# A repaired unit order (one table load counted per change) and shifted tokens made by products with identity matrices, in an eight-pair Mamba, expert, attention and window-attention kernel

## The chip, the cores and the metric

The kernel runs on one core of one Trainium2 chip. The metric is the device time in microseconds, the median of several executions. TensorE is called PE (its weight loads PEld), VectorE DVE, ScalarE ACT, GpSimd POOL and SyncE SP.

## The reference

A batch of 16 sequences of 256 tokens with 128 features passes two blocks. Cut to what matters:

```python
x = L0_attn_x                        # (16, 256, 128), float32
xn = layernorm(x)
x = x + mamba(xn) + moe(xn)          # selective scan (256 channels, 16 states); 8 experts, top 1
xn = layernorm(x)
x = x + geodesic_attention(xn)       # 16 heads of 8; softmax-like weights from arccos of cosines
      + window_transformer(xn)       # 2 layers, 8 heads of 64, window 64

def shift_token(t):                  # used twice in each layer of window_transformer
    t1, t2 = split(t, 2, axis=-1)    # 64 and 64 features
    t2 = pad(t2, one row of zeros ahead)[:-1]
    return concatenate([t1, t2], axis=-1)

def layer(x):
    h = shift_token(x); q, k, v = split(h @ wqkv)      # <- the shift that is changed
    x = x + window_attention(l2norm(q) * qs, l2norm(k) * ks, v) @ wo
    h = layernorm(shift_token(x)) * lg + lb
    a, g = split(h @ w1 + b1); return x + (a * gelu(g)) @ w2 + b2
```

## The kernel before

The 16 sequences are worked in 8 pairs of 512 tokens. The work is cut into units such as ("g_tan", pair, half, step): one stage of the computation on one pair or one sequence, issued on up to four engines. Names that begin with e are the experts, m the Mamba scan, f the join and second layernorm, g the geodesic attention; the units without a prefix (shift, qkv, norm, qn, heads, score, pt, rsum, pv, on, wo, ln, ln2, lnT, up, gelu, hid, down) are one window layer on one sequence. Pair 7's layers are 14 and 15, each with halves 0 and 1, one sequence each.

The order in which each engine meets the units is settled when the program is built. `schedule()` plays the units through a model of the five engines: `STAGES` holds the planner's own durations of a unit on each engine, `LATER` and `STREAM` add a wish (earlier or later) by the unit's name and by its stream (Mamba pair 3, say), and a free engine takes the ready unit with the lowest wish. On ACT a unit whose table of functions isn't loaded pays `SWITCH` in that choice and `LOAD_TIME` in the model's time. The resulting lists are then issued in order on each engine; semaphores alone set the times on the chip. All units of all pairs share eight PSUM banks, which the planner gives out too. What the planner believes has no other effect on the chip than the order and the banks.

ACT needs four tables: logarithm with exponential (most units), SILU (`m_in`), sigmoid with arctan (`g_tan`), GELU (`gelu`). `use()` at line 844 issues a load where the table changes. `g_tan` is Tanh then Arctan:

```python
use(SIG, GELU, SILU)       # loads the first of these unless one of them is there
a.activation(at, at, ACT.Tanh, scale=0.25)      # L1398
use(SIG)
a.activation(at, at, ACT.Arctan)                # L1401
```

The unit `shift` makes a layer's first operand, the shifted tokens with features on partitions: PE transposes the two 128-token tiles of a sequence (line 849, from `xn` in the first layer of a pair, `xd` in the second), and ACT copies them from PSUM to `hT1` in three instructions (lines 1431 to 1433): the 64 unshifted features, one column of zeros, the 64 others one token later. The `qkv` products (line 1153) read `hT1`. `m_scan` (line 1579) is the Mamba scan on DVE, 16 for each pair; `m_turn` (line 1357) is ACT's last copy of a pair's Mamba sums, two for each pair.

Of the kernel before, what the change touches and what calls it, by code (L numbers as in the profile page):

```python
# [10 lines left out]
P = 128  # L11
# [60 lines left out]
    "g_sub": [("POOL", 2.36)], "g_tan": [("ACT", 3.86)], "g_pow": [("ACT", 5.34)], "g_av": [("DVE", 0.53), ("PE", 1.0)],  # L72
    "g_ev": [("ACT", 0.6)], "g_avT": [("PE", 0.44), ("DVE", 1.05)], "g_oT": [("PE", 0.44), ("ACT", 0.6)],
    "g_out": [("PE", 0.89), ("DVE", 0.68)], "out": [("DVE", 0.69), ("SP", 0.1)],
    "shift": [("PE", 0.22), ("ACT", 0.97)], "norm": [("DVE", 0.17), ("ACT", 0.5)], "qn": [("DVE", 1.22)], "heads": [("PE", 0.88), ("ACT", 1.03)],
    "score": [("PE", 0.62), ("DVE", 0.61)], "pt": [("PE", 1.7), ("ACT", 0.7)], "rsum": [("PE", 0.65), ("ACT", 0.86)], "pv": [("PE", 1.15)], "on": [("DVE", 0.66)],
    "wo": [("PE", 1.83), ("DVE", 0.42)], "ln": [("PE", 0.69), ("DVE", 0.77), ("ACT", 0.54)],
    "ln2": [("DVE", 0.72)], "lnT": [("PE", 0.22), ("DVE", 0.54)], "up": [("PE", 0.86)], "gelu": [("ACT", 1.2)],
# [11 lines left out]
         "norm": "ln", "pt": "ln", "rsum": "ln", "ln": "ln", "m_in": "silu", "g_tan": "tan", "gelu": "gelu"}  # L90
SWITCH = 127.0

LATER = {"down": 17.13, "e_down": 0.92, "e_lg": -1373.3, "e_ln": 621.99, "e_load": -1698.97, "e_place": -129.783, "e_pre": 351.489,
         "e_route": 144.702, "e_scat": 829.618, "e_store": -223.789, "e_tr": -184.595, "e_up": 44.242, "e_xn": -28.591, "e_xt": -830.714,
         "f_ln": 818.98, "f_tr": -1660.36, "f_xn": -118.536, "f_yg": -111.816, "g_av": 89.144, "g_avT": -202.085, "g_ev": -784.392,
         "g_hd": -35.958, "g_ln": 938.103, "g_norm": -59.145, "g_oT": 238.89, "g_out": 718.35, "g_pow": 876.48, "g_qkv": 45.815,
         "g_score": 49.652, "g_sq": 72.566, "g_sub": 570.978, "g_tan": 44.449, "gelu": -343.785, "heads": 43.677, "hid": -127.469,
         "l_weights": 625.975, "ln": -124.928, "ln2": 1.634, "lnT": -15.963, "m_B": -153.424, "m_C": 17.261, "m_bx": 50.752,
         "m_dt": 18.917, "m_du": 21.175, "m_ex": -16.259, "m_fin": 74.245, "m_hc": 137.244, "m_in": -23.847, "m_load": -295.604,
         "m_out": -935.123, "m_scan": 731.575, "m_sum": 14.942, "m_turn": -247.837, "m_weights": -173.243, "m_xp": 895.808,  # L100
         "norm": -15.561, "on": -140.182, "out": 284.565, "pt": -39.622, "pv": 82.873, "qkv": 47.209, "qn": -65.566, "rsum": -2.347,
         "score": -4.24, "shift": -70.641, "up": -71.786, "wo": 25.239, "x_load": 44.744}

STREAM = {("-", 0): 147.932, ("e", 0): -62.078, ("e", 1): 166.105, ("e", 2): -162.027, ("e", 3): 122.427, ("e", 4): 496.972, ("e", 5): -233.745,
# [14 lines left out]

LOADED = [15.0, 24.0]  # L120

# [309 lines left out]
def schedule():  # L431
# [64 lines left out]
    while done < todo:  # L496
        for x in [y for y in waiting if y[0] <= now]:
            waiting.remove(x)
            offer(x[1], 0, now)
        again = True  # L500
        while again:
            again = False
            for e in engines:
                if free_at[e] > now:
                    continue
                best = None
                for x in engines[e]:
                    unit, stage, _ = x
                    if not may(unit, stage):
                        continue  # L510
                    needs = NEEDS.get(unit[0]) if e == "ACT" else None
                    cost = want[unit] + (SWITCH if needs and needs != table else 0)
                    if best is None or cost < best[0]:
                        best = (cost, x, needs)
                if best is None:
                    continue
                unit, stage, _ = x = best[1]
                engines[e].remove(x)
                taken.update(holds(unit)[0].get(stage, []))
                needs_banks = takes_banks(unit)  # L520
                if needs_banks and needs_banks[0] == stage:
                    banks[bank_of(unit)] = choose(unit, needs_banks[1])
                    for m, z in enumerate(banks[bank_of(unit)]):
                        idle.remove(z)
                        before_it[bank_of(unit), m] = held_by.get(z)
                        held_by[z] = (bank_of(unit), m)
                takes = stages(unit)[stage][1]
                if best[2] and best[2] != table:
                    takes += LOAD_TIME * (2 if best[2] == "tan" and table == "ln" else 1)
                    table = best[2]  # L530
                if e == "DVE" and unit[0] in DUAL:
                    takes += max(0.0, pool_until - now)
                    dual_until = now + takes
                if e == "POOL" and unit[0] in POOLED:
                    takes += max(0.0, dual_until - now)
                    pool_until = now + takes
                free_at[e] = now + takes
                plan[e].append(unit)
                line(unit, e).pop(0)
                events.append((now + takes + lands(unit, e), done, unit, stage))  # L540
                done += 1
                again = True
        times = [x for x in free_at.values() if x > now] + [x[0] for x in events + waiting]
        if not times:
            raise ValueError([(e, x[:3]) for e, x in engines.items()])
        now = min(times)
        for x in sorted(y for y in events if y[0] <= now):
            events.remove(x)
            finish(x[2], x[3], x[0])
# [31 lines left out]
def build(nc, d, out):  # L581
    ctx = ExitStack()
    with ctx:
# [263 lines left out]
        def transpose(out_, in_):  # L847
            k = in_.shape[0]
            return t.transpose(out_, in_, ident[0:k, 0:k])  # L849
# [101 lines left out]
        def tensor_program():  # L951
            for u, i, b, k in order(plan, "PE"):
# [183 lines left out]
                elif u == "shift":  # L1136
                    into(unit)
                    if l:
                        t.wait_ge(v_xd[b], n)
                    else:  # L1140
                        t.wait_ge(v_xn, n // LAY + 1)
                    for h in range(2):
                        e = transpose(lb()[:, h * P:(h + 1) * P], (xd if l else xn[n // LAY % 2])[:, 2 * b + h])
                    e.then_inc(p_sh[b], 1)
                    read_by(unit, a_hT[b], n + 1)
                elif u == "qkv":
                    if n == 0:
# [123 lines left out]
        def scalar_program():  # L1271
            for u, i, b, k in order(plan, "ACT"):
# [154 lines left out]
                elif u == "shift":  # L1427
                    a.wait_ge(p_sh[b], n + 1)
                    if n:
                        a.wait_ge(p_pt[b], 4 * n)  # L1430
                    a.activation(hT1[b][0:64], lb()[0:64, 0:L], ACT.Copy)
                    a.activation(hT1[b][64:128, 0:1], one_b[64:128, 0:1], ACT.Copy, scale=0.0)
                    a.activation(hT1[b][64:128, 1:L], lb()[64:128, 0:L - 1], ACT.Copy).then_inc(a_hT[b], 1)
                elif u == "qkv":
                    tt, w = divmod(k, 3)
                    a.wait_ge(p_q[b], 2 * (2 * n + tt) + w // 2 + 1)
# [601 lines left out]
```

## Time and profile before

| what | value |
|---|---|
| median of 3 runs | 2261.49 us (2258.05 to 2261.52) |
| the profiled execution | 2262.57 us, its span 2261.3 us |
| busy PE | 1788.6 us, 79% of the span |
| busy ACT | 1739.7 us, 77% |
| busy DVE | 1697.8 us, 75% |
| busy POOL | 541.0 us, 24% |
| mean granted clock of PE | 0.863 |

A busy share is the time in which the engine had an instruction under way. The span is the profiled execution without the 1.3 us around it. No engine is close to full, so no engine's sum of work alone sets the end: the rest is time in which an engine stands at the head of its list for something that another engine has not done yet.

### The profile page before, as it was taken

How to read it: one execution, taken by the hardware profiler on the slowest of the kernel's cores; microseconds unless marked ns; L12 is line 12 of the kernel's file. 1: busy time of each engine (PE TensorE's matmuls, PEld its weight loads, DVE VectorE, ACT ScalarE, POOL GpSimd, SP SyncE). 2: the span in 40 equal slices, each digit the busy share in tenths (PEclk: the TensorE clock that was granted, in tenths of full speed). 3: DMA queues.
4: the chain of work that ended last, by engine and by line, in shares of the span. 5: the costliest groups of instructions: out<-in, count | busy, mean ns of one | idle time of the engine just before them, and what ended most of it. 6: DMA issues, size and time to landing. Idle time of an engine off the chain costs nothing. (4 is left out here: it accounts for less than half of the span.)

```text
span 2261.3 us, 40539 instructions
## 1 busy us (share of the span) xinstructions
PE 1788.6 (79%) x15282; PEld 1293.3 (57%) x15282; DVE 1697.8 (75%) x2517; ACT 1739.7 (77%) x2887; POOL 541.0 (24%) x270
## 2 busy tenths in 40 slices
PE   3668788998778977788688887886778786779787
PEld 2654566776466654555465565554556464556565
DVE  4878887775999698859976889749984799655552
ACT  2435786857888697887878988977589958887996
POOL 2231122222311222312232222302142121232230
PEclk9687778999889888898788887998988888889888
DMA  6751214350341133114310233013300242000000
GB/s 227 237 170 48 71 38 135 117 147 18 127 136 52 53 117 108 43 39 131 113 39 14 73 122 103 10 49 121 130 21 2 84 141 84 1 1 2 6 1 6
DMA packets 81651, 177.39 MB, mean 78 GB/s; under 512 B 10388, under 2 KB 41940, under 8 KB 81332
## 3 DMA queue, kind: packets, MB, share of 16 engines
q1 hardware_dynamic: 75632, 163.53, 22.4%
q0 software_dynamic: 2816, 7.21, 1.0%
q10 hardware_dynamic: 3012, 4.06, 0.5%
q8 instruction: 125, 2.05, 0.4%
q14 instruction: 66, 0.54, 0.1%
HBM read 161.92 MB, written 12.85 MB: 77 GB/s over the span
## 5 line engine op out<-in xcount | busy, mean ns | idle before, releaser
L1855 POOL TENSOR_TENSOR arena<-arena 128x1024 f32<-128x1024 f32 x128 | 316.3, 2493 | 622.8 <-ACT arena L1392 622.6
L1859 POOL TENSOR_TENSOR arena<-arena,rb 128x1024 f32<-128x1024 f32 x64 | 152.2, 2378 | 866.5 <-DVE rb L1711 866.5
L1579 DVE TENSOR_TENSOR_SCAN ps<-dA,ps 128x1024 f32<-128x1024 f32 x128 | 291.0, 2284 | 1.6 <-ACT dA L1351 1.0
L1153 PE MATMUL ps<-w_l_wqkv,arena 128*128 128x512 f32 x384 | 205.8, 670 | 23.0 <-DVE hB L1587 6.4
L844 ACT ACT_TABLE_LOAD x153 | 196.3, 1283 | 19.3 <-issue 16.6
L1413 ACT ACTIVATE arena<-arena 128x256 f32<-128x256 f32 x512 | 205.3, 402 | 2.0
L1351 ACT ACTIVATE dA<-mv,w_A_log 128x510 f32<-128x510 f32 x256 | 167.8, 711 | 42.2 <-DVE ps L1579 39.1
L1093 PE MATMUL ps<-gqT,gkT 8*128 8x256 f32 x1024 | 164.7, 460 | 38.9 <-DVE arena L1652 16.1
L1652 DVE TENSOR_SCALAR arena<-ps 128x1024 f32<-128x1024 f32 x128 | 155.0, 1217 | 51.3 <-PE ps L1093 50.7
L1573 DVE TENSOR_TENSOR ps<-BC,mv 128x1024 f32<-128x1024 f32 x128 | 181.6, 1425 | 12.9 <-ACT arena L1457 4.1
L849 PE MATMUL ps<-w_ident,arena 128*128 128x128 f32 x623 | 112.1, 326 | 99.5 <-DVE arena L1512 28.6
L1043 PE MATMUL ps<-w_ident,hB 128*128 128x128 f32 x1024 | 162.4, 312 | 28.7 <-DVE hB L1587 28.6
L1043 PEld LDWEIGHTS ps<-w_ident,hB 128*128 128x128 f32 x1024 | 136.5, 162 | 54.4 <-DVE hB L1587 33.2
L1729 DVE TENSOR_REDUCE nmx<-ps 128x4 f32<-128x512 f32 x128 | 87.8, 686 | 97.8 <-PE ps L1181 97.2
L849 PEld LDWEIGHTS ps<-w_ident,arena 128*128 128x128 f32 x623 | 87.2, 169 | 125.0 <-issue 83.2
L1587 DVE TENSOR_TENSOR hB<-ps,BC 128x1024 f32<-128x1024 f32 x128 | 154.4, 1214 | 4.4 <-PE ps L1043 3.6
L1093 PEld LDWEIGHTS ps<-gqT,gkT 8*128 8x128 f32 x1024 | 101.0, 213 | 80.4 <-issue 70.4
L1192 PE MATMUL ps<-arena 64*128 64x192 f32 (+1 forms) x1024 | 118.5, 352 | 35.1 <-DVE rb L1711 13.9
L1390 ACT ACTIVATE arena<-arena,one_b 128x2048 f32<-128x2048 f32 x64 | 127.7, 1996 | 22.8 <-DVE arena L1652 20.9
L1192 PEld LDWEIGHTS ps<-arena 64*128 64x128 f32 x1024 | 92.5, 207 | 83.8 <-issue 49.9
L1153 PEld LDWEIGHTS ps<-w_l_wqkv,arena 128*128 128x128 f32 x384 | 74.4, 211 | 101.9 <-issue 94.1
L1392 ACT ACTIVATE arena<-arena,one_b 128x2048 f32<-128x2048 f32 x64 | 128.2, 2003 | 2.1
(223 smaller groups left out, 4507.7 us busy)
## 6 DMA issues: line engine op xcount, KB each, us to landing
BC<-bc_d SPq DMA_DIRECT2D x224, 512.0 KB, 4.2
BC<-in_experts SPq DMA_DIRECT2D x16, 514.0 KB
arena<-in_experts SPq DMA_DIRECT2D x15, 514.0 KB
mv<-in_experts SPq DMA_DIRECT2D x15, 514.0 KB, 3.4
arena<-in_x SPq DMA_DIRECT2D x8, 256.0 KB, 4.7
xnT_d<-arena SPq DMA_DIRECT2D x8, 256.0 KB, 3.0
hB<-xnT_d SPq DMA_DIRECT2D x8, 256.0 KB, 2.6
x<-in_x SPq DMA_DIRECT2D x8, 256.0 KB, 5.6
```

The costliest lines, as they stand in the source:

```text
L844: a.preload_act_table_set(names[0])
L849: return t.transpose(out_, in_, ident[0:k, 0:k])
L1043: e = t.matmul(lb()[:, tt * P:(tt + 1) * P], hB[k % 2][:, j, tt * P:(tt + 1) * P], ident, is_transpose=True, start=q == j == tt == 0, stop ...
L1093: e = t.matmul(lb(z)[:, kt * L:(kt + 1) * L], gkT[32 * hi:32 * hi + GD, hb, kt * P:(kt + 1) * P], gqT[32 * hi:32 * hi + GD, hb], start=Tru ...
L1153: e = t.matmul(lb(z), hT1[b][:, tt * P:(tt + 1) * P], w_lqkv[:, l, (w + z) * INNER:(w + z + 1) * INNER], start=True, stop=True)
L1192: t.matmul(lb(z)[:, cols], kT[head_rows(z), k, at:at + P], qT[head_rows(z), k, at:at + cols.stop - cols.start], start=kt == 0, stop=False)
L1351: e = a.activation(dA[k % 2][:, j].rearrange("p (s l) -> p s l", s=2)[:, :, 1:], dtv[:, c].rearrange("p (s l) -> p s l", s=2)[:, :, 1:], A ...
L1413: e = a.activation(part, part, ACT.Exp, scale=-3.2, accum_out=vt[m % 2][:, kt, hi, GD + 2:GD + 3])
L1573: v.tensor_tensor(two_banks(unit), Bb[j % 2], bc(du[:, c:c + 1], [P, NG, T]), ALU.mult).then_inc(v_bx, 1)
L1579: v.tensor_tensor_scan(h_, flat2(dA[k % 2]), h_, 0.0, ALU.mult, ALU.add).then_inc(v_scan, 1)
L1652: v.tensor_scalar(cl[m % 2][:, 2 * (k % 2):2 * (k % 2) + 2], two_banks(unit), -1.0 + 1e-7, 1.0 - 1e-7, ALU.max, ALU.min).then_inc(v_gs, 1)
L1855: g.tensor_tensor(la[m % 2][:, half], la[m % 2][:, half], cl[m % 2][:, half], ALU.subtract).then_inc(g_sub, 1)
```

## The change

Three things change. First, `shift` on PE: in place of two transposes there are four products of 64 features by 128 tokens, two with the identity (features 0 to 63) and two with the identity moved by one column, `w_next` (features 64 to 127, one token later), and one product with one column, which adds at token 128 what the first tile's last token owes the second. Second, the zeros and the shift are then in PSUM already, and ACT empties it with a single copy of 128x256. Third, the planner: its durations of `shift` change, it counts one `LOAD_TIME` for any change of table (before, two for one from the logarithm's table to `g_tan`), and `LATER` and `STREAM` have new numbers throughout.

```diff
-    "shift": [("PE", 0.22), ("ACT", 0.97)], ...
+    "shift": [("PE", 0.55), ("ACT", 0.4)], ...

-LATER = {"down": 17.13, "e_down": 0.92, "e_lg": -1373.3, ...
+LATER = {"down": 26.626, "e_down": -47.853, "e_lg": -154.046, ...

                 if best[2] and best[2] != table:
-                    takes += LOAD_TIME * (2 if best[2] == "tan" and table == "ln" else 1)
+                    takes += LOAD_TIME
                     table = best[2]

+                    rows = xd if l else xn[n // LAY % 2]
                     for h in range(2):
-                        e = transpose(lb()[:, h * P:(h + 1) * P], (xd if l else xn[n // LAY % 2])[:, 2 * b + h])
-                    e.then_inc(p_sh[b], 1)
+                        for z, moved in ((0, ident), (1, w_next)):
+                            t.matmul(lb()[head_rows(z), h * P:(h + 1) * P], rows[:, 2 * b + h, 64 * z:64 * z + 64], moved, start=True, stop=True)
+                    t.matmul(lb()[head_rows(1), P:P + 1], rows[:, 2 * b, 64:128], ident[:, P - 1:P], start=False, stop=True,
+                             skip_group_check=True).then_inc(p_sh[b], 1)

-                    a.activation(hT1[b][0:64], lb()[0:64, 0:L], ACT.Copy)
-                    a.activation(hT1[b][64:128, 0:1], one_b[64:128, 0:1], ACT.Copy, scale=0.0)
-                    a.activation(hT1[b][64:128, 1:L], lb()[64:128, 0:L - 1], ACT.Copy).then_inc(a_hT[b], 1)
+                    a.activation(hT1[b], lb()[:, 0:L], ACT.Copy).then_inc(a_hT[b], 1)
```

Lines behind the PE edit stand three higher in the changed kernel (two from ACT's `shift` on to one): the old L1398 is L1401, the old L1484 is L1485.

The new order touches every engine from its first microseconds on. Three places of it follow. The first is on PE, the last `shift` of the program (layer 15, half 1; `xd` is the residual stream of the window layers). Before:

```order
L1181 MATMUL ps<-arena 64x128 x4
L849 MATMUL ps<-w_ident,xd 128x128 x2
L1224 MATMUL ps<-arena 32x192 x2
L1224 MATMUL ps<-PT,arena 32x192 x2
L1224 MATMUL ps<-arena 32x128 x2
```

In the changed kernel:

```order
L1268 MATMUL ps<-w_l_w,arena 128x128 x6
L1145 MATMUL ps<-w_ident,xd 64x128 x4
L1146 MATMUL ps<-w_ident,xd 64x1
L1156 MATMUL ps<-w_l_wqkv,arena 128x512 x6
L1107 MATMUL ps<-arena,vt 32x256 x8
```

The two transposes became four products and a fifth with one column, and the `qkv` products now follow at once, where others stood between.

The second place is on ACT around the last copy of the Mamba sums (`mv<-ps 128x512`, `m_turn` of pair 7), behind which the program holds no Mamba work on ACT. Before:

```order
L1465 ACTIVATE arena<-ps 128x640
L1357 ACTIVATE mv<-ps 128x512
L1439 ACTIVATE arena<-ps 128x1024
L1408 ACTIVATE arena<-arena,one_b 128x2048
L1413 ACTIVATE arena,vt<-arena 128x256 x8
L1465 ACTIVATE PT<-ps 128x640
```

In the changed kernel:

```order
L1466 ACTIVATE arena<-ps 128x640
L1434 ACTIVATE arena<-ps 128x256
L1360 ACTIVATE mv<-ps 128x512
L1393 ACTIVATE arena<-arena,one_b 128x2048
L1395 ACTIVATE arena<-arena,one_b 128x2048
L1425 ACTIVATE avS<-ps 128x512
```

Counted in the whole order, ACT had 361 instructions behind that copy and has 287 now. The difference by kind: 24 fewer of L1413 (104 to 80), 11 fewer with 2048 columns (12 to 10 each of L1390, L1392, L1398 and L1401, 13 to 10 of L1408), 8 fewer table loads (27 to 19), 11 fewer of `shift` (5 times three to 4 of one), and 20 fewer short ones. In the same way DVE has 280 instructions behind its last scan (318 before), and PE 1295 behind its last Mamba sum, line 1043 (1514 before). Over the whole program the table loads are 164 (153 before), and all other instructions of ACT and DVE but those of `shift` are as many as before; PE has 96 more.

The third place is ACT again, the last two `g_tan` pairs (L1398 and L1401) of the program. Before:

```order
L844 ACT_TABLE_LOAD
L1398 ACTIVATE arena<-arena 128x2048
L1401 ACTIVATE arena<-arena 128x2048
L844 ACT_TABLE_LOAD
L1484 ACTIVATE arena<-ps,w_l_b 128x256 x2
L1484 ACTIVATE arena<-ps,w_l_b 87x256
L844 ACT_TABLE_LOAD
L1465 ACTIVATE arena<-ps 128x640
L844 ACT_TABLE_LOAD
L1398 ACTIVATE arena<-arena 128x2048
L1401 ACTIVATE arena<-arena 128x2048
L844 ACT_TABLE_LOAD
```

In the changed kernel (numbers as above):

```order
L844 ACT_TABLE_LOAD
L1401 ACTIVATE arena<-arena 128x2048
L1404 ACTIVATE arena<-arena 128x2048
L1401 ACTIVATE arena<-arena 128x2048
L1404 ACTIVATE arena<-arena 128x2048
L844 ACT_TABLE_LOAD
L1466 ACTIVATE arena<-ps 128x640 x2
L1411 ACTIVATE arena<-arena,one_b 128x2048
```

Here two `g_tan` share one load and the GELU has gone behind them. Over the whole program it is the other way: 25 times two `g_tan` stood together before, 17 times now.

## Rows read from the trace of the kernel before

**Rows 1.** The page: busy time by engine, and two rows by slices

```profile
PE 1788.6 (79%) x15282; PEld 1293.3 (57%) x15282; DVE 1697.8 (75%) x2517; ACT 1739.7 (77%) x2887; POOL 541.0 (24%) x270
...
DVE  4878887775999698859976889749984799655552
ACT  2435786857888697887878988977589958887996
```

**Rows 2.** The page: the chain of work that ended last, by engine

```profile
PE 6%; ACT 6%; DVE 2%; issue 1%; DVEq 0%; ACTq 0%
```

**Rows 3.** Last Mamba scan on DVE, last Mamba copy on ACT: ns, first to last start

```profile
L1579 DVE TENSOR_TENSOR_SCAN ps<-dA,ps x128: 2261/2285/2296, 64.7 to 1910.7; 128x1024 f32<-128x1024 f32 x128
...
L1357 ACT ACTIVATE mv<-ps x16: 574/594/599, 159.5 to 1927.2; 128x512 f32<-128x512 f32 x16
```

**Rows 4.** Busy us (instructions) of PE, PEld, DVE, ACT, POOL; clock; DMA

```profile
0.00:1927.20 1927.20, 1521.96 (x12726) 1100.12 (x12728) 1528.35 (x2209) 1460.78 (x2422) 455.94 (x235) 0.86 0.28 92
1927.20:2261.30 334.10, 266.62 (x2558) 193.21 (x2558) 169.45 (x309) 278.94 (x467) 85.05 (x35) 0.87 0.01 3
...
0.00:1913.00 1913.00, 1508.99 (x12620) 1093.12 (x12620) 1520.92 (x2200) 1452.60 (x2399) 453.58 (x234) 0.86 0.29 92
1913.00:2261.30 348.30, 279.58 (x2662) 200.21 (x2662) 176.88 (x318) 287.12 (x489) 87.41 (x36) 0.86 0.01 3
```

**Rows 5.** Groups on ACT from 1927.2 us on: busy us, mean ns

```profile
L1413 ACT ACTIVATE arena<-arena 128x256 f32<-128x256 f32 x104 | 41.7, 402 | 0.4
L844 ACT ACT_TABLE_LOAD x27 | 34.6, 1283 | 0.5
L1408 ACT ACTIVATE arena<-arena,one_b 128x2048 f32<-128x2048 f32 x13 | 25.9, 1993 | 0.0
...
L1401 ACT ACTIVATE arena<-arena 128x2048 f32<-128x2048 f32 x12 | 22.9, 1910 | 0.4
...
L1465 ACT ACTIVATE PT<-ps 128x640 f32<-128x640 f32 x13 | 9.1, 697 | 2.8 <-PE ps L1202 2.8
```

**Rows 6.** Groups of the whole run: table loads, shift's copies, a 128x256 copy

```profile
L844 ACT ACT_TABLE_LOAD x153 | 196.3, 1283 | 19.3 <-issue 16.6
...
L1470 ACT ACTIVATE arena<-ps 128x256 f32<-128x256 f32 x64 | 24.3, 380 | 24.2 <-PE ps L1212 23.4
...
L1433 ACT ACTIVATE arena<-ps 64x255 f32<-64x255 f32 x32 | 12.1, 378 | 0.4
L1431 ACT ACTIVATE arena<-ps 64x256 f32<-64x256 f32 x32 | 11.8, 368 | 9.8 <-PE ps L849 9.8
...
L1432 ACT ACTIVATE arena<-one_b 64x1 f32<-64x1 f32 x32 | 6.4, 200 | 0.4
```

**Rows 7.** Timeline of PE at a shift: start us, us

```profile
1000.99 0.38 PE L849 MATMUL ps<-w_ident,xn 128*128 128x128 f32 x2
...
1001.65 0.28 PE L1212 MATMUL ps<-arena,one_b 128*32 128x128 f32 x2
1001.67 0.28 PE L1212 MATMUL ps<-PT,one_b 128*32 128x128 f32 x2
1001.76 0.28 PE L1212 MATMUL ps<-arena,one_b 128*32 128x128 f32 x2
```

**Rows 8.** Timeline of ACT near the end, around table loads

```profile
2212.01 1.91 ACT L1401 ACTIVATE arena<-arena 128x2048 f32<-128x2048 f32 x1
2213.94 1.28 ACT L844 ACT_TABLE_LOAD   x1
2215.23 1.19 ACT L1484 ACTIVATE arena<-ps,w_l_b 128x256 f32<-128x256 f32 x3
2216.44 1.28 ACT L844 ACT_TABLE_LOAD   x1
2217.74 0.70 ACT L1465 ACTIVATE arena<-ps 128x640 f32<-128x640 f32 x1
2218.46 1.28 ACT L844 ACT_TABLE_LOAD   x1
```

More of the change, by code:

```diff
@@ L74 @@
     "g_out": [("PE", 0.89), ("DVE", 0.68)], "out": [("DVE", 0.69), ("SP", 0.1)],
-    "shift": [("PE", 0.22), ("ACT", 0.97)], "norm": [("DVE", 0.17), ("ACT", 0.5)], "qn": [("DVE", 1.22)], "heads": [("PE", 0.88), ("ACT", 1.03)],
+    "shift": [("PE", 0.55), ("ACT", 0.4)], "norm": [("DVE", 0.17), ("ACT", 0.5)], "qn": [("DVE", 1.22)], "heads": [("PE", 0.88), ("ACT", 1.03)],
     "score": [("PE", 0.62), ("DVE", 0.61)], "pt": [("PE", 1.7), ("ACT", 0.7)], "rsum": [("PE", 0.65), ("ACT", 0.86)], "pv": [("PE", 1.15)], "on": [("DVE", 0.66)],
@@ L91 @@
 SWITCH = 127.0
[L93 to L102, printed above, removed]
@@ L104 @@
-STREAM = {("-", 0): 147.932, ("e", 0): -62.078, ("e", 1): 166.105, ("e", 2): -162.027, ("e", 3): 122.427, ("e", 4): 496.972, ("e", 5): -233.745,
[14 rows of a table removed]
+LATER = {"down": 26.626, "e_down": -47.853, "e_lg": -154.046, "e_ln": 153.128, "e_load": -413.903, "e_place": 198.432, "e_pre": 372.282,
+         "e_route": 78.833, "e_scat": -133.57, "e_store": 294.029, "e_tr": -401.726, "e_up": 10.066, "e_xn": 93.952, "e_xt": -1039.55,
+         "f_ln": 1106.4, "f_tr": -322.455, "f_xn": 217.43, "f_yg": -10.994, "g_av": 97.117, "g_avT": -642.248, "g_ev": -451.117,
+         "g_hd": -107.765, "g_ln": 1286.07, "g_norm": -120.908, "g_oT": 944.286, "g_out": 190.596, "g_pow": 1280.3, "g_qkv": 64.332,
+         "g_score": 50.079, "g_sq": -142.519, "g_sub": -7.947, "g_tan": 70.185, "gelu": -544.024, "heads": 50.193, "hid": -284.193,
+         "l_weights": -54.396, "ln": -431.199, "ln2": -432.525, "lnT": -137.825, "m_B": 7.171, "m_C": -955.695, "m_bx": 42.085,
+         "m_dt": 96.366, "m_du": 297.038, "m_ex": 43.637, "m_fin": 159.803, "m_hc": 143.75, "m_in": 21.962, "m_load": 701.197,
+         "m_out": -718.386, "m_scan": 2376.5, "m_sum": 25.023, "m_turn": -358.511, "m_weights": 139.751, "m_xp": 1472.38,
+         "norm": -295.405, "on": -852.033, "out": -519.201, "pt": -305.656, "pv": 88.73, "qkv": 44.395, "qn": -533.45, "rsum": -13.76,
+         "score": -11.158, "shift": -205.939, "up": -112.371, "wo": 36.793, "x_load": 100.085}
@@ L120 @@
+STREAM = {("-", 0): -58.238, ("e", 0): -221.022, ("e", 1): 1263.18, ("e", 2): -232.508, ("e", 3): 325.479, ("e", 4): 68.616, ("e", 5): -262.222,
[14 rows of a table added]
 LOADED = [15.0, 24.0]
```

28 rows, old and new, of the table STREAM are left out of this document.

## The prediction

> **What bounds the kernel now.** I read the page first. PE, ACT and DVE are busy 79%, 77% and 75% of the span [rows 1], and the chain that ended last is held by PE 6%, ACT 6% and DVE 2% [rows 2], so it covers only the last stretch and can't be charged with the whole. The reader should see three engines, each a quarter idle, that wait for each other; no single wait is long enough to be named as the bound. What varies is the mix: in the slices DVE stands at 9 up to the middle and falls to 5 and 2 at the end, where ACT stands at 9 [rows 1].
>
> So I looked for the place where the mix changes. The last Mamba scan starts at 1910.7 us and takes 2.3, so it ends at 1913.0; ACT's last copy of Mamba sums starts at 1927.2 [rows 3]. Splitting the run there gives the two regimes [rows 4]. Up to 1927.2 us ACT is busy 1460.78 us, a share of 0.758, and PE 1521.96, or 0.790; up to 1913.0 DVE is busy 1520.92, or 0.795. Behind 1927.2 there are 334.1 us in which ACT is busy 278.94, a share of 0.835, PE 266.62 (0.798), but DVE only 169.45 (0.51). The tail is ACT's, with PE close; DVE, which has all the scans, has little left. An order that brings attention and window work forward, beside the scans, shortens the tail. One that puts it off lengthens it.
>
> **The shift, ACT's part.** Three instructions of 368, 200 and 378 ns fall away, 0.946 us, and one 128x256 copy from PSUM comes, whose nearest row is L1470 with the same shape and 380 ns [rows 6]. That is 0.566 us less for each of 32 shifts: -18.1 us of ACT's work.
>
> **The shift, PE's part.** Two transposes ran in 0.38 us together [rows 7]. The four products aren't in the trace in this form. The nearest row is L1212, products with 128 rows into 32 columns of the array: of four such at 128 columns the first start at 1001.65 and the next set at 1001.76 [rows 7], so neighbours in different columns of the array go side by side, a set every 0.11 us. If the two halves pair up like that, two sets take what two transposes took, and only the one-column product is new, some 0.04 us: +1.3 us over 32. If they don't, two more steps of 0.11 and one of at most 0.11 come: 0.33 us each, +10.6. They write different columns of the array as L1212 does, so I take a value near the lower end, 3 us. On the path of one shift (0.38 and 0.95 before qkv can start, against 0.4 to 0.7 and 0.38) it can't lose; I book nothing for it beyond ACT's busy time, as another unit of PE usually stands ready in between.
>
> **The planner's count of loads.** The edit to LOAD_TIME removes no load from the chip. Already now g_tan is preceded by one load, and Arctan by none. What reaches the chip is the new numbers' order. It has 164 loads for 153: 11 at 1.283 us [rows 6] are +14.1 us of ACT's work. With the shift, ACT's total goes by -4.0 us: alone, no change worth measuring.
>
> Here a rule speaks against the change. In the trace a load costs its own duration and no more: it starts at 2216.44, lasts 1.28, and the next instruction starts at 2217.74; the three at 2213.94 to 2218.46 are all like that [rows 8]. The Trainium skill, page ScalarE: Activation LUTs, section What ACT_TABLE_LOAD costs, adds a drain of about 1.38 us to each change of set, 2.66 us in all, and advises grouping by set. By that price, an estimate from that page, the 11 loads would be 29 us and not 14. The trace does not agree.
>
> **The tail.** Behind ACT's last Mamba copy the order holds 361 instructions before and 287 after. The itemised difference: 24 of L1413 at 0.402 are 9.6 us; 8 loads at 1.283 are 10.3; 11 with 2048 columns at 1.91 to 1.99 are 21.5 [rows 5]; the shifts fall from 5 x 0.946 to 4 x 0.38, 3.2 us [rows 6]; the 20 short ones lie between the 0.2 us of the smallest row and 1.0, with L1465 at 0.697 the commonest [rows 5, 6], and I take 0.55 each, 11.0. Together 55.6 us. ACT's tail is then 278.9 - 55.6 = 223.3 us busy, and at the same share of 0.835 it lasts 267.4 in place of 334.1: **-66.7 us**.
>
> **What is paid ahead of it.** That work has not gone; it stands beside the scans. ACT's part before its last Mamba copy grows by 55.6 - 4.0 = 51.6 us; at its share of 0.758, +68 us. DVE has 280 instructions behind its last scan for 318; at 176.88 us for the 318 [rows 4] that is 21 us moved forward, at 0.795 +27 us. PE has 1295 behind its last sum for 1514; 266.62 us [rows 4] scaled so is 38.5 us, with the shift's 3 some 42, at 0.790 +53 us. Were ACT alone to set the pace ahead, the scans would end 68 us later; were DVE, 27. The shares ahead are nearly alike on all three, none of them sets the pace alone, so I take the mean of the three, (68 + 27 + 53) / 3 = **+49 us**.
>
> **Sum.** 49 - 67 = -18 us against the profiled 2262.6 gives 2244.6. That execution lay 1.1 us above the median of the runs, so I forecast 2243. Its own range, from the spread of that mean and from 3 to 10.6 us on PE, is 2230 to 2256.
>
> **Rivals.**
> 1. *Much faster, because the shares themselves rise.* The planner's picture of ACT was wrong before: 35 changes from the logarithm's table to g_tan were counted double, some 45 us of loads that the chip never does (35 x 1.283) [rows 6]. With a true picture, units may be placed where they are really ready. If ACT ahead of the tail were at 0.775 in place of 0.758, its 1512.4 us there would take 1951, and with 267 the total would be 2218. For it: the 0.835 of the tail shows that ACT can be denser. Against: the waits on the chip are a few microseconds each and come from PE, DVE and PSUM as much as from ACT. 2205 to 2229.
> 2. *Slower: ACT sets the pace ahead, and PE the tail.* ACT takes the 11 more loads and the moved work, and the scans end +68 us later. In the tail PE is next after ACT: its 266.6 us shrink to 228, at 0.798 286 us, or -48. The sum is +20, 2282. It decides when ACT holds up the scans: each scan needs m_ex from ACT (L1351). What speaks for it is that 145 loads stand ahead of the last Mamba copy where 126 stood, in the stretch where ACT has to serve the scans; what speaks against it is that DVE is denser than ACT there. It turns from gain to loss when the scans end more than 67 us late. 2266 to 2290.
> 3. *No change*: ACT alone sets both stretches. +68 - 67 is +1, 2262, within 0.2% (4.5 us, about what a measurement of this kernel can tell from none).
>
> By the page's price above, the 19 more loads ahead of the tail and 8 fewer behind would make rival 2 the likelier one: the 11 x 1.38 would add 15 us to my forecast, 2258. The rows give it no support, and I leave it 3 in 100, within rivals 2 and 3.
>
> **How the numbers follow.** The forecast 0.50; rival 1 0.17; rival 2 0.20; rival 3 0.13. Faster is the forecast with rival 1, less the little of it above 2257: 0.66. Same 0.13, slower 0.21. The range is 2208 to 2272: it leaves out about 0.05 of rival 1 below and 0.13 of rival 2 above.
>
> **What would show it.** In the changed profile: L1434 at about 380 ns 32 times, and L1145 sets that start 0.11 us apart (right) or single products 0.11 apart each (PE's cost of 10.6). 164 loads of 1283 ns, each followed at once by the next instruction. ACT's busy time near 1736 us, DVE's unchanged. The last L1580 scan near 1950 us with 267 us behind ACT's last L1360, in place of 334; a scan end beyond 1995 us makes the forecast wrong and rival 2 right, one at 1920 or earlier speaks for rival 1. ACT's share ahead of that copy tells the two apart: 0.76 for the forecast, 0.775 or more for rival 1, 0.75 or less for rival 2. The forecast is also wrong if the tail's share falls: its 223 us busy of ACT stretched beyond 290.

## Result, and the profile after

The changed kernel takes 2146.4 us in the median (2141.5 to 2160.8, 4 runs) against 2261.3: a ratio of 0.951, 95% interval 0.946 to 0.955. The forecast was 2243; the side was right, the size was missed by far, and the time lies 62 us below the range.

The page of the changed kernel, busy time by engine and the same two rows by slices as in [rows 1]:

```profile
PE 1730.9 (81%) x15538; PEld 1268.6 (59%) x15538; DVE 1684.1 (79%) x2517; ACT 1727.3 (81%) x2834; POOL 541.9 (25%) x270
...
DVE  4968998766899799877997699878997699777363
ACT  2534798858996478898998999888999898978986
```

The work is nearly what it was: ACT 12 us less, DVE 14 less, PE 58 less though it has more instructions. The span lost 121 us: on ACT 109 and on DVE 107 of them are time in which the engine stood idle, on PE 63. The 58 us that PE is busy less go with its clock: the granted clock was 0.863 before and is 0.894, and 1788.6 x 0.863 / 0.894 is 1727. The reader should compare the middle of the rows: ACT stood mostly at 7 and 8 there and now stands mostly at 8 and 9.

Last starts of the Mamba scan and of ACT's last Mamba copy, as in [rows 3]:

```profile
L1580 DVE TENSOR_TENSOR_SCAN ps<-dA,ps x128: 2259/2284/2296, 64.4 to 1852.8; 128x1024 f32<-128x1024 f32 x128
...
L1360 ACT ACTIVATE mv<-ps x16: 578/594/603, 161.4 to 1865.8; 128x512 f32<-128x512 f32 x16
```

The split at that copy, and at the end of the last scan, as in [rows 4], columns the same:

```profile
0.00:1865.80 1865.80, 1507.55 (x13352) 1108.91 (x13356) 1534.30 (x2251) 1503.29 (x2466) 471.28 (x240) 0.89 0.29 95
1865.80:2140.20 274.40, 223.32 (x2190) 159.66 (x2190) 149.82 (x266) 223.98 (x369) 70.58 (x30) 0.90 0.01 3
0.00:1855.10 1855.10, 1499.24 (x13254) 1102.55 (x13255) 1528.15 (x2237) 1492.71 (x2440) 471.28 (x240) 0.89 0.29 95
```

The tail lasts 274 us with ACT busy 224.0; the prediction had 267 with 223.3. Ahead of it ACT does 1503.3 us of work, as predicted (1512), but in 1866 us, where I had 1976: a share of 0.806 and not 0.765. All of the miss is there. The other two engines are denser there too: PE has 0.808 for 0.790, DVE up to the end of its last scan 0.824 for 0.795.

The longest waits of ACT before (us in total, times, longest):

```profile
ACT arena L1439 <- PE ps L1153: 55.5, 30, 6.3
ACT arena L1465 <- PE ps L1202: 39.9, 20, 7.8
ACT dA L1351 <- DVE ps L1579: 39.1, 25, 4.3
ACT PT L1465 <- PE ps L1202: 36.9, 23, 4.2
ACT arena L1457 <- PE ps L849: 34.6, 25, 4.7
```

and of the changed kernel:

```profile
ACT PT L1466 <- PE ps L1205: 43.9, 24, 5.3
ACT arena L1466 <- PE ps L1205: 33.4, 17, 7.0
ACT arena L1440 <- PE ps L1156: 27.5, 23, 2.7
...
ACT dA L1354 <- DVE ps L1580: 21.6, 19, 2.6
...
ACT arena L1458 <- PE ps L849: 19.8, 15, 4.8
```

The lines stand one to three higher there (L1439 is L1440). None of the five vanished; three about halved (55.5 to 27.5, 39.1 to 21.6, 34.6 to 19.8), one fell a little (39.9 to 33.4) and one grew (36.9 to 43.9). Together they give 60 of the 109 us of idle time that ACT lost. A better order looks like this: many waits of one to five microseconds, fewer in number and shorter each.

### The profile page after: what moved, and what is told of

Read it like the earlier page. It is cut to its first block and busy times, and to the rows that moved or that the text cites. A ratio compares the mean times of both kernels' runs of the same rounds, so it can differ in the third digit from the quotient of the medians.

```text
span 2140.2 us, 40998 instructions
## 1 busy us (share of the span) xinstructions
PE 1730.9 (81%) x15538; PEld 1268.6 (59%) x15538; DVE 1684.1 (79%) x2517; ACT 1727.3 (81%) x2834; POOL 541.9 (25%) x270
## 5 line engine op out<-in xcount | busy, mean ns | idle before, releaser
L844 ACT ACT_TABLE_LOAD x164 | 210.4, 1283 | 18.8 <-issue 15.9
L1156 PE MATMUL ps<-w_l_wqkv,arena 128*128 128x512 f32 x384 | 196.5, 639 | 23.2 <-DVE hB L1588 6.5
L1354 ACT ACTIVATE dA<-mv,w_A_log 128x510 f32<-128x510 f32 x256 | 168.7, 713 | 21.9 <-DVE ps L1580 21.6
L1093 PE MATMUL ps<-gqT,gkT 8*128 8x256 f32 x1024 | 155.2, 439 | 38.5 <-DVE arena L1653 15.1
L1653 DVE TENSOR_SCALAR arena<-ps 128x1024 f32<-128x1024 f32 x128 | 154.8, 1216 | 34.0 <-PE ps L1093 33.4
L1043 PE MATMUL ps<-w_ident,hB 128*128 128x128 f32 x1024 | 150.2, 295 | 23.7 <-DVE hB L1588 18.4
L1043 PEld LDWEIGHTS ps<-w_ident,hB 128*128 128x128 f32 x1024 | 126.4, 153 | 50.2 <-issue 25.2
L1093 PEld LDWEIGHTS ps<-gqT,gkT 8*128 8x128 f32 x1024 | 96.1, 204 | 75.3 <-issue 66.4
L1393 ACT ACTIVATE arena<-arena,one_b 128x2048 f32<-128x2048 f32 x64 | 127.7, 1995 | 10.5 <-DVE arena L1653 9.0
L1395 ACT ACTIVATE arena<-arena,one_b 128x2048 f32<-128x2048 f32 x64 | 128.2, 2003 | 2.1
L1411 ACT ACTIVATE arena<-arena,one_b 128x2048 f32<-128x2048 f32 x64 | 127.6, 1994 | 0.1
```

Of the source, the lines that this page charges most:

```text
L844: a.preload_act_table_set(names[0])
L1043: e = t.matmul(lb()[:, tt * P:(tt + 1) * P], hB[k % 2][:, j, tt * P:(tt + 1) * P], ident, is_transpose=True, start=q == j == tt == 0, stop ...
L1093: e = t.matmul(lb(z)[:, kt * L:(kt + 1) * L], gkT[32 * hi:32 * hi + GD, hb, kt * P:(kt + 1) * P], gqT[32 * hi:32 * hi + GD, hb], start=Tru ...
L1156: e = t.matmul(lb(z), hT1[b][:, tt * P:(tt + 1) * P], w_lqkv[:, l, (w + z) * INNER:(w + z + 1) * INNER], start=True, stop=True)
L1354: e = a.activation(dA[k % 2][:, j].rearrange("p (s l) -> p s l", s=2)[:, :, 1:], dtv[:, c].rearrange("p (s l) -> p s l", s=2)[:, :, 1:], A ...
```

## Experiments

Sixteen kernels ran, each beside the kernel before on the same chip. In these later comparisons the kernel before took 2249 to 2252 us, so the ratios, not the microseconds, compare across them: the changed kernel's 0.9506 is 2138 us there.

**e1, one line.** The planner of the kernel before counts one load for each change of table; nothing else.

```diff
-                    takes += LOAD_TIME * (2 if best[2] == "tan" and table == "ln" else 1)
+                    takes += LOAD_TIME
```

> The kernel before with a single edit: the planner counts one LOAD_TIME for every change of table, as the changed kernel does. The old wishes (LATER, STREAM), the old shift and its old planner costs stay. The order differs from the kernel before from the first window layer on; it has 155 table loads (before 153, changed kernel 164). Theory FIT (the wishes in LATER and STREAM are fitted to one exact set of planner costs, the old wishes to one load per change; any other cost scrambles the order): this line alone gives most of the gain, 2130 to 2165 us. Theory SEARCH (the new wishes are simply better ones, and the old ones are as good as they get): a small change either way, 2240 to 2275. Theory SHIFT (the gain comes from the shorter shift): 2255 to 2270, no change.

Measured: 2180.8 us, ratio 0.968 (0.965 to 0.972). This line reaches the chip only through the order (and the PSUM banks that the planner gives out with it), and it gives two thirds of the gain with the old wishes and the old shift. SEARCH and SHIFT are out as sole causes; FIT is right in kind, 16 us short of its range. The split at the end of the last scan, columns as in [rows 4]:

```profile
0.00:1884.10 1884.10, 1517.65 (x12838) 1104.87 (x12839) 1534.80 (x2223) 1486.47 (x2458) 464.01 (x239) 0.86 0.29 94
1884.10:2185.90 301.80, 246.44 (x2446) 177.76 (x2444) 167.61 (x295) 251.35 (x432) 73.09 (x31) 0.89 0.01 3
```

Both parts shrank: the scans end at 1884 (before 1913), the tail is 302 us (before 348). ACT's share ahead of that end is 0.789 (before 0.759), though its work in the whole run is the same within 2 us.

**e2, the shift alone.** The program edit of `shift` as in the change, the planner untouched.

```diff
-                        e = transpose(lb()[:, h * P:(h + 1) * P], (xd if l else xn[n // LAY % 2])[:, 2 * b + h])
+                            t.matmul(lb()[head_rows(z), h * P:(h + 1) * P], rows[:, 2 * b + h, 64 * z:64 * z + 64], moved, start=True, stop=True)
...
+                    a.activation(hT1[b], lb()[:, 0:L], ACT.Copy).then_inc(a_hT[b], 1)
```

> The kernel before with the program edit of shift alone (four products and a one-column product on PE, one copy on ACT); the planner is untouched, so every unit stands where it stood before. Theory SHIFT: a clear gain, 2140 to 2200. Theories FIT and SEARCH: ACT has 18 us less to do but none of it binds everywhere, so 0 to 15 us less, 2246 to 2261.

Measured: 2247.3 us, ratio 0.9985 (0.9969 to 1.0002): no difference that can be told from none.

**e3, the order alone.** The changed kernel with the old transposes and three copies in the program, the inverse of e2's edit, every unit where the changed kernel has it.

> The changed kernel with the old shift in the program (two transposes, three copies), in the changed kernel's order. Theory SHIFT: back near 2260. Theories FIT and SEARCH: nearly all of the gain stays; ACT has 18 us more to do in a denser order, 2148 to 2166.

Measured: 2142.4 us, ratio 0.9515 (0.9487 to 0.9544). The whole gain stays. ACT is busy 1749.3 us here, 22 more than in the changed kernel, at a cost of 2 us, give or take 12. The split at the end of its last scan:

```profile
0.00:1856.30 1856.30, 1500.04 (x13038) 1095.46 (x13039) 1530.26 (x2237) 1511.85 (x2494) 468.96 (x240) 0.89 0.30 95
```

With the old shift ACT has a share of 0.814 here.

**e4, a nudge.**

```diff
-"hid": -284.193, ... "qkv": 44.395,
+"hid": -284.193, ... "qkv": 44.695,
```

> The changed kernel with one wish moved by 0.3 of over 2000 (LATER of qkv 44.395 to 44.695), which the planner turns into another order from the second window layer on (179 table loads for 164; 150 units of ACT behind the last Mamba copy for 132). All planner costs stay as true as in the changed kernel. Theory FIT: the gain is a property of this one order, not of the costs, and a neighbour is an ordinary order: 2215 to 2270. Theory TRUE PICTURE (the gain comes because the planner now counts loads as the chip does): the neighbour keeps most of it, 2145 to 2185.

Measured: 2220.4 us, ratio 0.988 (0.984 to 0.993), as FIT had it. The same costs, one wish moved by 0.3, and three quarters of the gain are gone. The split at the end of its last scan:

```profile
0.00:1869.00 1869.00, 1482.67 (x12772) 1082.54 (x12772) 1514.10 (x2200) 1475.74 (x2404) 455.55 (x234) 0.88 0.30 94
1869.00:2213.00 344.00, 276.75 (x2766) 201.07 (x2766) 180.39 (x318) 274.29 (x446) 85.99 (x36) 0.89 0.01 3
```

The scans end early here too, but with less beside them, and the tail is as long as in the kernel before (348). So an order can win one of the two stretches and lose the other. The nudged order also has 15 more table loads (179 for 164), some 19 us more work on ACT; the loss is some 85 us, so they are the smaller part of it.

**e5 to e7, more work on one engine at a time**, order of the changed kernel.

```diff
                     use(LN_EXP)
+                    a.preload_act_table_set(LN_EXP)          # e5, in g_pow
...
+                    if k % 2 == 0:                           # e6, in g_score on DVE
+                        v.tensor_reduce(idle_out[:, m], two_banks(unit), AX.X, ALU.max)
...
-                    for kt in range(2):                      # e7, in g_score on PE
+                    for kt in (0, 1, 0, 1)[:4 if k % 2 == 0 else 2]:
```

> The changed kernel with a second, needless load of the logarithm's table ahead of each of the 64 g_pow units; the order is unchanged. ACT has 64 x 1.283 = 82 us more to do. Theory MEAN (the prediction's step: the three engines share the pace and one engine's work counts a third ahead of the tail): 82/3 divided by 0.8, about +30 to +45 us, 2175 to 2190. Theory ACT BINDS: +75 to +100, 2220 to 2245. Theory SLACK (ACT's idle fifth absorbs it): under +20, below 2165. By the Trainium skill's price of 2.66 us for a change of set (page ScalarE: Activation LUTs, section What ACT_TABLE_LOAD costs), an estimate from that page, ACT would have 170 us more and the time would pass 2260.

> The changed kernel with one more DVE reduction over 128x1024 elements in PSUM (about 1.2 us, nothing reads its result) ahead of the clamp in each of the 64 even g_score units; order unchanged. DVE has about 78 us more. Theory MEAN: +25 to +45, 2172 to 2190. Theory DVE BINDS ahead of the tail: +70 to +90. Theory SLACK: under +20.

> The changed kernel with the four score products of each of the 64 even g_score units issued twice (same operands, same place); order unchanged. PE has some 64 x 0.5 to 1.0 = 32 to 64 us more. Theory MEAN: +12 to +30, 2158 to 2176. Theory PE BINDS: +40 to +70. Theory SLACK: under +12.

Measured: e5 2198.8 us (ratio 0.979, 0.976 to 0.982), e6 2186.9 (0.973, 0.971 to 0.975), e7 2190.4 (0.975, 0.973 to 0.978). Only 57 of e5's 64 loads are in the program: in the other seven places `use()` issues a load of the same table directly ahead, and the trace has one load there, not two. The extra work in e5 and e6:

```profile
L1410 ACT ACT_TABLE_LOAD  x57: 1283/1283/1283, 258.8 to 2159.2; - x57
```

```profile
L1655 DVE TENSOR_REDUCE idle_out<-ps x64: 1192/1216/1226, 214.8 to 2093.3; 128x2 f32<-128x1024 f32 x64
```

For e7 the group of the repeated products is compared with the same group in e5, which ran at nearly the same granted clock (0.882, e7 0.881):

```profile
L1093 PE MATMUL ps<-gqT,gkT 8*128 8x256 f32 x1024 | 160.5, 450 | 34.3 <-DVE arena L1654 12.6 <-DVE rb L1713 6.8 <-DVE hB L1589 6.4
```

```profile
L1093 PE MATMUL ps<-gqT,gkT 8*128 8x256 f32 x1536 | 228.9, 450 | 30.2 <-DVE arena L1653 8.6 <-DVE rb L1712 8.3 <-DVE hB L1588 5.8
```

| | work added, us | time added, by the ratios, us | quotient |
|---|---|---|---|
| e5 ACT | 57 x 1.283 = 73 | 64 | 0.9 |
| e6 DVE | 64 x 1.216 = 78 | 50 | 0.6 |
| e7 PE | 228.9 - 160.5 = 68 | 55 | 0.8 |

(The intervals of the ratios make each time uncertain by some 12 us, the quotients by 0.2.) MEAN, the step of the prediction, expected 0.33 / 0.8 = 0.4 for each; only e6 comes near it. None binds alone, none has slack. Together they are 2.3: in the dense order a delay on any engine is handed on to the others, which the picture of three independent shares can't give. Two limits: all three ran at a mean granted clock of 0.881 where the changed kernel had 0.890, and some 9 us of each time go with that (worked out under "Open"). And the quotient is that of work put at this place: e3's 22 us more on ACT, in the shifts, cost 2 us, give or take 12.

**e8 and e11, the count changed in mid-program.** The kernel before with two loads counted only behind (e8) or only ahead of (e11) the middle of the planner's time.

```diff
-LOAD_TIME * (2 if best[2] == "tan" and table == "ln" else 1)
+LOAD_TIME * (2 if best[2] == "tan" and table == "ln" and now > 1066 else 1)     # e8; e11: now <= 1066
```

> The kernel before, where the planner counts one load per change in the first half of its own time and two for logarithm to g_tan in the second. Its order is that of e1 up to the middle and goes its own way behind it. Theory FIT (each stretch is as good as its match to the wishes): half of the loss of the kernel before against e1, about 2215. Theory TAIL (what matters is how the last pair ends): all of the loss is there, 2240 to 2260. Theory FRONT (the loss is made early and stays): 2180 to 2195, as e1.

> The mirror of e8: the kernel before, with two loads counted for logarithm to g_tan in the first half of the planner's time and one in the second. The order is that of the kernel before up to the middle. Theory FIT, in which it is the whole chain of choices that was fitted: a true count behind a scattered first half meets wishes that were fitted to other states and gives little, 2220 to 2250. Theory STRETCH (each half is as good as its own count): half of the gain of e1, about 2215.

Measured: e8 2231.3 us, ratio 0.993 (0.991 to 0.996); e11 2237.1, 0.995 (0.993 to 0.997). e8 keeps e1's whole first half and only a fifth of e1's gain. In e11 a true count in the second half behind the old first half is worth 12 us of e1's 69. So the two halves don't add up: 18 and 12 us for 69. STRETCH, TAIL and FRONT fall, TAIL by 9 us only. FIT had e11 right, but for e8 it had about 2215, and the time came 16 us above that: FIT says which orders are poor, not by how much.

**e12, the shift in the order of e1.** e1's line and e2's edit together.

> The order of e1 (old wishes, one load per change, old planner costs of shift) with the new shift in the program. It says what the shift edit is worth in a dense order. Theory SHIFT COUNTS WHEN DENSE (ACT's work counts three quarters there, by e5): 0.75 x 18 us less on ACT and some microseconds more on PE, 5 to 12 us below e1, 2168 to 2176. Theory SHIFT NEVER COUNTS: 2178 to 2184. e1 stood 40 us above the changed kernel though both orders came of fitted wishes; if this run closes that gap, the gap was the shift.

Measured: 2151.2 us, ratio 0.958 (0.954 to 0.961), by the ratios 24 us below e1 (0.968), give or take 11. The time lies below both expected ranges. The same edit is worth 0.15% in the order before, 0.1% in the changed kernel's (e3 against it) and 1.1% in e1's, the last two give or take 0.5%. By e5's quotient 18 us less work on ACT would give 16, which the interval allows; in e3 the same work cost next to nothing. What it removes here isn't settled. In the profiled executions the granted clock of PE is 0.881 where e1 has 0.868, and PE is busy 1753 us for 1764.

**e9, e10, e13 to e16, the wishes searched anew.** The numbers in `LATER` and `STREAM` were changed at random, one to three at a time, some 18,000 times, and kept where the planner's own end came earlier. e9 keeps the kernel before's program; the others have the changed kernel's program and start from the old wishes. e9, e13 and e14 count two loads from logarithm to g_tan, e10, e15 and e16 one:

```diff
-LATER = {"down": 17.13, "e_down": 0.92, ...
+LATER = ...        # as searched
...
-                    takes += LOAD_TIME                       # e13, e14
+                    takes += LOAD_TIME * (2 if best[2] == "tan" and table == "ln" else 1)
```

> The kernel before, old shift and the false count (two loads from logarithm to g_tan) kept; only the numbers in LATER and STREAM were searched anew, some 18,000 random changes of one to three wishes kept where the planner's own end came earlier. 161 table loads. Theory TRUE PICTURE (the planner must count loads as the chip does): the false count still misplaces 37 of them, 2225 to 2260. Theory FIT (the count itself does little harm; what the kernel before lacks is wishes fitted to the count it uses): most of the gain comes, 2155 to 2200.

> The changed kernel (new shift, one load per change) with other wishes: the old ones of the kernel before as the start, and the same number of random changes as in e9. Its first order, without the search, would be as scattered as that of e4. Theory FIT: within 1 per cent of e9 and near the changed kernel, 2150 to 2190. Theory TRUE PICTURE: 2150 to 2190 too, but 2 per cent or more below e9. Theory LUCK (the changed kernel's order happened to suit the chip, another one doesn't): 2200 to 2240.

> As e10 (changed kernel's program, planner costs of the new shift, old wishes searched anew with as many random changes), but the planner counts two loads from logarithm to g_tan. It differs from e10 in that count and what the search made of it alone; 156 loads, the count is false at 33 places. Theory TRUE PICTURE: like e9, 2200 to 2235. Theory LUCK (e9 was an unlucky order, and orders spread by a per cent either way): 2140 to 2180.

> A second search of the same kind as e13 with other random changes; 153 loads, false at 34 places. TRUE PICTURE: 2200 to 2240. LUCK: anywhere from 2140 to 2225, unlike e13.

> A second search of the kind of e10 (one load per change); 156 loads. TRUE PICTURE: 2135 to 2165. LUCK: anywhere from 2135 to 2225.

> A third search of the kind of e10, whose planner's end stayed 0.8 per cent later than that of e10; 156 loads. TRUE PICTURE, with the chip following the planner's end: 2150 to 2185. LUCK: anywhere from 2135 to 2225.

| wishes | count of loads | ratio to the kernel before | planner's own end, us |
|---|---|---|---|
| fitted: the changed kernel | true | 0.951 (0.946 to 0.955) | 2134 |
| e1, the old wishes | true | 0.968 (0.965 to 0.972) | 2132 |
| searched anew: e10 | true | 0.951 (0.948 to 0.955) | 2148 |
| e15 | true | 0.970 (0.965 to 0.976) | 2152 |
| e16 | true | 0.966 (0.963 to 0.969) | 2165 |
| searched anew: e13 | false | 0.965 (0.963 to 0.967) | 2175 |
| e14 | false | 0.982 (0.979 to 0.985) | 2186 |
| e9 | false | 0.989 (0.986 to 0.992) | 2191 |
| not fitted to the costs: e4 | true | 0.988 (0.984 to 0.993) | 2223 |
| e8, e11 | half and half | 0.993, 0.995 | 2219, 2209 |
| the kernel before | false | 1 | 2248 |

The last column is no measurement: it is the time at which `schedule()` of each kernel, played without the chip, finishes its last unit. It shows what the runs alone leave open, that the old wishes do fit a planner that counts one load. With them and that count the planner ends at 2132 us, as early as with the changed kernel's wishes (2134); with the count of two at 2248. Only part of this is the time of the loads that the chip never does: the order of the kernel before, played once more with one load each, still ends at 2227. The searched orders end between 2132 and 2191, the others at 2209 or later. On the chip a single order lies between 10 us below and 48 us above that end (e10, e1), so the column ranks the two kinds of order and not single ones.

e13 alone refutes the strict TRUE PICTURE: with the count false at 33 places a searched order still is 3.5% faster. e15 and e16 refute that a true count ensures the best: the chip spreads 2% over orders that the search left near each other (e10 and e15, whose ends lie 4 us apart). e9 and e10 alone would have misled: 4% apart, it looked like the count. With all in, orders with a true count average 0.961 (five), with a false one 0.978 (three), those whose wishes were not fitted 0.988 and up. That the false count costs a further percent or two after a search is likely but, with e13 below e15, not shown.

For the last scan, e10 and e9 differ as the changed kernel and the kernel before did. e10:

```profile
L1557 DVE TENSOR_TENSOR_SCAN ps<-dA,ps x128: 2261/2286/2296, 65.2 to 1852.9; 128x1024 f32<-128x1024 f32 x128
```

and e9:

```profile
L1556 DVE TENSOR_TENSOR_SCAN ps<-dA,ps x128: 2261/2286/2296, 66.4 to 1916.5; 128x1024 f32<-128x1024 f32 x128
```

## Why the prediction was right or wrong

**The split into two regimes and the tail: right.** ACT's work behind its last Mamba copy was forecast at 223.3 us and is 224.0, its share there 0.835 and is 0.816, its length 267 and is 274.

**"What is paid ahead of it": wrong, the step that failed.** The prediction's +49 us there was in truth -61: ACT's last Mamba copy came at 1866 us, before at 1927. I took each engine's share ahead of the tail as a constant (0.758, 0.795, 0.790), divided the moved work by it and took the mean. The moved work was right within 10 us, the shares were not constants: ACT's is 0.806, and the copy comes at 1866 where the sum gave 1976. A share is a result of the order, and the order was replaced. e1 and e3 show that the order alone moves it, with the work as it was (ACT's share up to the end of the last scan: 0.759 before, 0.789 in e1, 0.814 in e3); e5 to e7 show the second fault, that engines which wait for each other don't each carry a third.

**"The edit to LOAD_TIME ... What reaches the chip is the new numbers' order": half wrong.** It removes no load, true, but the line reorders the program with the numbers as they were, and that alone is 3.2% (e1). The wishes and the costs are one thing: the old wishes fit a planner that counts one load, as its own end shows (2132 us). The kernel before paired them with a count of two and so had an order that was not fitted to its costs. The diff and `use()` showed the contradiction; I counted it as 45 us of loads that the planner only believes in, in rival 1. I also never played `schedule()` for its end: 2248 against 2134 us would have spoken for a large gain before any run. That this difference of 115 us is also the measured one is luck, as e1 shows, which the planner has 48 us too early. A smaller misreading: Arctan is preceded by no load in 60 of 64 places, not in all; in four Tanh runs with another table, and the load stands between the two.

**Rival 1 was the case that came, for half of its reason and at a third of its size.** I gave it 0.17 and 2205 to 2229. The shares did rise, but less through the true count as such than through fitted wishes (e4 with true costs 0.988, e13 with a false count 0.965).

**The shift.** ACT's copy: 0.38 us expected, and so it is (0.36 to 0.42). On PE the timeline of the changed kernel shows one of the first shifts, at the upper level of the clock (granted 1.00 in this stretch), and the last one, at the lower level (0.50); start, us:

```profile
294.31 0.66 PE L1145 MATMUL ps<-w_ident,xd 128*64 128x128 f32 x8
294.81 0.23 PE L1146 MATMUL ps<-w_ident,xd 128*64 128x1 f32 x2
...
2054.13 1.12 PE L1145 MATMUL ps<-w_ident,xd 128*64 128x128 f32 x8 [0.60 <-DVE xd L1768]
...
2055.04 0.32 PE L1146 MATMUL ps<-w_ident,xd 128*64 128x1 f32 x2
2055.46 0.37 ACT L1434 ACTIVATE arena<-ps 128x256 f32<-128x256 f32 x1
2055.85 1.28 ACT L844 ACT_TABLE_LOAD   x1
```

Four products are eight entries, two each, where a transpose of float32 is one. The halves do go side by side (their entries start 6 ns apart), but there are four sets and not two. From the first start to the last end a shift takes 0.72 us at the upper level, where two transposes took 0.38 to 0.44. So PE's price is the upper bound of some 0.33 us for each shift, 10.6 in all, and not the 3 us that I took; for my 0.04 us for the product with one column no row spoke, and it is two entries as well. It made no difference to the sum: in the order before (e2) and the changed kernel's (e3) the whole edit of the shift is worth nothing that can be measured; in e1's (e12) it is worth more.

**Table loads.** 164 came, at 1283 ns each. By the Trainium skill, page ScalarE: Activation LUTs, section What ACT_TABLE_LOAD costs, a change of set takes 2.66 us in all. The trace of the changed kernel doesn't agree: behind 151 of the 163 loads that follow on other work the next instruction starts within 1.31 us of the load's start, and the load itself mostly starts 18 ns behind the end of the instruction before it. So 2.66 us for each has no support here. e5's loads change no set, so they don't test that price; 57 of them added 64 us, 1.1 each, and the profile shows the next instruction at once:

```profile
258.76 1.28 ACT L1410 ACT_TABLE_LOAD   x1
260.06 2.00 ACT L1412 ACTIVATE arena<-arena,one_b 128x2048 f32<-128x2048 f32 x1
```

**Rivals 2 and 3**: my mark for a loss was a last scan that ends beyond 1995 us; it started at 1853, which is beyond my mark for rival 1 (1920 or earlier) too. The 11 more loads were real, 14 us, and small beside the 109 us of idle time that ACT lost.

**Open.** The granted clock goes with the time: 0.863 before, 0.868 in e1, 0.859 in e9, 0.894 in the changed kernel, 0.897 in e10. It goes with it inside one kernel too, where the order is the same: over 118 executions (the changed kernel, e1 to e16 and the kernel before beside them), each set against the mean of its own kernel, 0.01 more clock comes with 10 us less time (8 to 12). The changed kernel's four executions have a mean clock of 0.890, the 39 later ones of the kernel before 0.867. At that rate 23 of some 111 us would go with the clock, an estimate from these rows, and some 90 would be left at an equal clock. Whether a denser order lifts the clock or a clock that stays up makes the order dense was not tried. Open too is which units' places close which waits: the runs show that the order does it, not which part of it.

## What to carry to other kernels

Where a searched order rests on a model's costs, costs and searched numbers are one object: a change of either, however small or true, gave an unfitted order here, 2 to 5% slower (e4, e8, e11, the kernel before), and whoever corrects a cost has to search again before measuring the correction. When a diff replaces the whole order, don't carry busy shares over from the old trace; play the planner of both kernels for its own end, which needs no chip; widen the range by what the waits could give back, and look whether the old order was fitted to the costs it stands beside. And compare several orders, not one with one: two equally searched ones lay 2% apart, as much as most edits bring.

## What the runs showed of the hardware that was not expected

A load of the table that is already there costs its full 1283 ns (e5). Two float32 products into the two halves of the array's columns run side by side, but each is two entries in the profile, where a float32 transpose is one (the timeline of L1145 above, eight entries for four products, against x2 for two transposes in [rows 7]). The same shift took 0.72 us on PE where the granted clock was 1.00 and 1.23 us where it was 0.50.
